# Graph network, four layers on one core: a 16-bit running table in the ranking, a longer late part, and 2 KB lines in the third node stage

## The reference, cut to what matters

```python
h = jnp.maximum(_layernorm(x, axis=-1), 0.0)
x = x + _L0_gnn_ref(h, edge_index, ...)   # needs scores[e] = a_s.h[src] + a_t.h[dst]
h = jnp.maximum(_layernorm(x, axis=-1), 0.0)
x = x + _L1_gnn_ref(h, src, dst, edge_weight, ...)
h = jnp.maximum(_layernorm(x, axis=-1), 0.0)
x = x + _L2_gnn_ref(h, src, dst, ...)     # softmax over the edges of one src, then sum into dst
h = jnp.maximum(_layernorm(x, axis=-1), 0.0)
x = x + _L3_gnn_ref(h, edge_index, edge_attr_2, ...)
```

## Time and profile before

| what | us |
|---|---|
| median of 3 runs (7792.51 to 7794.23) | 7792.8 |
| the profiled execution | 7779.12 |
| its span | 7777.4 |
| ranking: loop over 392 tiles, about 837 to 1409 | 572 |
| ranking: late part, about 1409 to 1523 | 114 |
| ranking: POOL alone, about 1523 to 1565 | 42 |
| node pass 2, about 3616 to 4475 | 859 |

### The profile page before, as it was taken

The page is one execution under the profiler, slowest core; times in us unless marked ns, Lnnn a source line. Parts: engine busy times, 40 slices in busy tenths (PEclk is TensorE's granted clock), DMA queues, the critical chain, the costliest instruction groups (busy, mean ns, idle before and its releaser), DMA issues. The chain is left out here.

```text
span 7777.4 us, 155361 instructions
## 1 busy us (share of the span) xinstructions
PE 5839.5 (75%) x23114; PEld 3656.9 (47%) x23115; DVE 5209.4 (67%) x18189; ACT 3315.6 (43%) x9563; POOL 3876.2 (50%) x4972
## 2 busy tenths in 40 slices
PE   4997999847779997677999967777686779400477
PEld 3774344336634443554444445555335668300365
DVE  5999777745579995455666656666784569533765
ACT  1993355205545552344444445454222557300155
POOL 1556777700022224766766677777460013577443
PEclk7999999979999998999999989999899999755799
DMA  2664333559867775787999866666208978422177
GB/s 59 211 211 129 101 104 103 170 164 337 307 213 247 249 248 196 248 309 259 308 305 306 290 196 205 204 204 202 63 7 280 339 252 228 130 54 55 50 234 249
DMA packets 970395, 1560.51 MB, mean 201 GB/s; under 512 B 125352, under 2 KB 736925, under 8 KB 970246
## 3 DMA queue, kind: packets, MB, share of 16 engines
q1 hardware_dynamic: 654502, 860.68, 33.7%
q10 hardware_dynamic: 188000, 410.91, 15.2%
q0 software_dynamic: 127744, 287.44, 13.5%
HBM read 861.17 MB, written 697.48 MB: 200 GB/s over the span
## 5 line engine op out<-in xcount | busy, mean ns | idle before, releaser
L2128 PE MATMUL node_p_out<-w,node_h_t 128*128 128x512 f32 (+2 forms) x6272 | 2176.8, 470 | 13.1 <-ACT node_h_t L2164 12.3
L1434 PE MATMUL merge_banks<-merge_rows,merge_mask 128*128 x6264 | 1537.5, 401 | 538.5 <-SPq L1365 139.8
L1434 PEld LDWEIGHTS merge_banks<-merge_rows,merge_mask 128*128 128x128 f32 x6264 | 1204.8, 198 | 871.2 <-issue 710.5
L1416 DVE TENSOR_SCALAR merge_mask<-ramp,dst_at,soft_at_step 128x128 f32<-128x128 f32 x2349 | 822.9, 353 | 778.0 <-PE merge_banks L1434 623.9
L2128 PEld LDWEIGHTS node_p_out<-w,node_h_t 128*128 128x128 f32 x6272 | 1013.9, 191 | 452.8 <-issue 396.9
L2041 POOL TENSOR_TENSOR node_inv_std<-node_var,node_minus_half 128x4 f32<-128x4 f32 x392 | 434.1, 1107 | 1428.9 <-DVE node_var L1926 857.4
L1498 ACT COPY merge_total<-merge_banks 128x512 f32<-128x512 f32 x784 | 458.1, 584 | 1097.0 <-PE merge_banks L1434 1014.4
L2106 PE MATMUL node_p_turn<-ident,node_xn 128*128 128x128 f32 x3136 | 620.6, 280 | 219.0 <-DVE node_xn L1933 116.4
L2106 PEld LDWEIGHTS node_p_turn<-ident,node_xn 128*128 128x128 f32 x3136 | 404.6, 141 | 768.2 <-issue 476.3
L2164 ACT ACTIVATE node_h_t<-node_p_turn 128x256 f32<-128x256 f32 x1568 | 601.3, 383 | 229.3 <-PE node_p_turn L2106 223.6
L1485 ACT COPY merge_banks<-merge_held 128x512 f32<-128x512 f32 x784 | 461.4, 589 | 228.2 <-PE merge_banks L1424 114.9
(11 more groups left out here) (564 smaller groups left out, 11073.3 us busy)
## 6 DMA issues: line engine op xcount, KB each, us to landing
merge_held<-own ACTq DMA_DIRECT2D x196, 512.0 KB, 6.0
x<-merge_total ACTq DMA_DIRECT2D x196, 512.0 KB, 4.3
node_x<-x SPq DMA_DIRECT2D x196, 512.0 KB, 6.1
node_x<-in_x SPq DMA_DIRECT2D x194, 512.0 KB
merge_rows<-h_by_edge SPq DMA_DIRECT2D x408, 128.0 KB, 4.2
merge_rows<-by_edge SPq DMA_DIRECT2D x408, 128.0 KB, 3.7
h<-node_rows_h SPq DMA_DIRECT2D x98, 516.0 KB, 4.2
h_by_edge<-rank_src_of_src SPq DMA_DIRECT2D x49, 1024.0 KB, 4.6
```

The source lines that it names most:

```text
L1416: ins = nc.vector.tensor_scalar(mask[j][:], k.ramp[:, 0:P], columns(k.dst_at, s), columns(weight, s), ALU.is_equal, ALU.mult)
L1434: nc.tensor.matmul(banks[:, bass.ds(nc.s_assert_within(at[2 * j + 1], 0, (BANKS - 1) * 512, skip_runtime_bounds_check_because=small), D)], ...
L2128: ins = nc.tensor.matmul(p_out[w][g % banks][:, 0:n], h_t[g][:, c * P:(c + 1) * P], matrix[:, c, :], start=c == 0, stop=c == 1)
```

## The change

In the loop the float32 snapshot and float32 look-up are replaced: `coarse` holds the table rounded to 16 bits (two copies, by block), `p_run` holds what is left over, which is small enough to be exact in 16 bits. `rank` becomes three 16-bit matmuls, and `copies` makes one 16-bit copy that `match` and `rank` both use. Before the first tile of each block DVE does three operations in a row (`take_apart`): add coarse to `p_run`, round the sum into the other coarse, put the difference back into `p_run`. `snap` of that tile waits for it. LATE goes from 15 to 19 blocks (152 tiles). The splitting of the late keys moves from ahead of the histogram to behind the loop. In node pass 2 `normalize` writes into `out`, where it stands beside the first product, and one DMA stores both as lines of 2 KB.

```diff
-    LATE = 15 * U
+    LATE = 19 * U
...
+            chain(nc.vector.tensor_tensor(whole, below[:], p_rank[1][:, 0:NTH], ALU.subtract))
+            chain(nc.vector.tensor_copy(coarse_of(0), whole))
             dve.sem_inc(prefix, 1)
+            nc.vector.tensor_tensor(p_run[:, 0:NTH], whole, coarse_of(0), ALU.subtract).then_inc(rebased, 1)
...
+            def take_apart(t, j):
+
+                if j or (isinstance(t, int) and t == 0):
+                    return
+                dve.wait_ge(added, t)
+                nc.vector.tensor_tensor(whole, p_run[:, 0:NTH], coarse_of(t - U), ALU.add).then_inc(rejoined, 1)
+                dve.wait_ge(rejoined, block_of_tile(t))
+                if not (isinstance(t, int) and t == U):
+                    dve.wait_ge(ranked, t - U)
+                nc.vector.tensor_copy(coarse_of(t), whole).then_inc(parted, 1)
+                dve.wait_ge(parted, block_of_tile(t))
+                nc.vector.tensor_tensor(p_run[:, 0:NTH], whole, coarse_of(t), ALU.subtract).then_inc(rebased, 1)
+
+            walk(dve, [(0, head), (2, before_in_tile), (2, take_apart), (4, pick)])
...
-                nc.tensor.matmul(p_rank[j % 2][:, 0:NTH], low_t[j][:], starts[j % FOUR][:], start=True, stop=False)
+                nc.tensor.matmul(p_rank[j % 2][:, 0:NTH], low_t[j][:], coarse_of(t), start=True, stop=False)
+                nc.tensor.matmul(p_rank[j % 2][:, 0:NTH], low_t[j][:], starts[j % FOUR][:], start=False, stop=False)
...
             def snap(t, j):
                 after(act, added, t)
+                if j == 0:
+                    act.wait_ge(rebased, block_of_tile(t) + 1)
                 after(act, ranked, t - FOUR + 1)
...
             def copies(t, j):
                 act.wait_ge(turned, t + 1)
-                after(act, same, t - FOUR + 1)
-                nc.scalar.copy(low_tb[j % FOUR][:], p_turn[j % 2][:, 0:P]).then_inc(copied_b, 1)
                 after(act, ranked, t - U + 1)
                 nc.scalar.copy(low_t[j][:], p_turn[j % 2][:, 0:P]).then_inc(copied, 1)
...
-                    parts = [out[q.h][:, n] for n in range(2)] + [biased[q.h][:], xn[q.h][:]]
+                    parts = [out[q.h][:, :, 0:2, :].rearrange("p g n f -> p g (n f)"), out[q.h][:, :, 2, :], biased[q.h][:]]
...
-                        nc.scalar.copy(out[q.h][:, 0:2, g, :], p_out[0][g % banks][:].rearrange("p (n f) -> p n f", n=2)
+                        nc.scalar.copy(out[q.h][:, g, 0::2, :], p_out[0][g % banks][:].rearrange("p (n f) -> p n f", n=2)
...
-        node_pass(nc, k, 2, x2, tables=(pair2[:, 0:D], to_dst, own2, pair2[:, D:2 * D]))
+        node_pass(nc, k, 2, x2, tables=(pair2, to_dst, own2))
```

More of the change, by code:

```diff
@@ L408, in rank_sources @@
     at_high = [ph.sb(f"at_high{n}", [P, NTH], BF16) for n in range(U)]
-    low_t = [ph.sb(f"low_t{n}", [P, P]) for n in range(U)]
-    low_tb = [ph.sb(f"low_tb{n}", [P, P], BF16) for n in range(FOUR)]
+    low_t = [ph.sb(f"low_t{n}", [P, P], F16) for n in range(U)]
     earlier = [ph.sb(f"earlier{n}", [P, P], BF16) for n in range(FOUR)]
-    starts = [ph.sb(f"starts{n}", [P, NTH]) for n in range(FOUR)]
-    counts, below, upto, zeros = starts
+    starts = [ph.sb(f"starts{n}", [P, NTH], F16) for n in range(FOUR)]
+    coarse = ph.sb("coarse", [P, 2 * NTH], F16)
+    scratch = ph.sb("scratch", [P, 4 * NTH])
+    late_low_t = [scratch[:, n * P:(n + 1) * P] for n in range(U)]
+    whole = scratch[:, 3 * NTH:4 * NTH]
+    counts, below, upto, zeros = (scratch[:, n * NTH:(n + 1) * NTH] for n in range(4))
     picked = [ph.sb(f"picked{n}", [P, NTH], BF16) for n in range(2)]
@@ L551, in pick @@
                     nc.vector.tensor_copy(columns(pos_out, t - U + 1, U), rank_f[:]).then_inc(rank_kept, 1)
-            walk(dve, [(0, head), (2, before_in_tile), (4, pick)])
+            def take_apart(t, j):
[10 more added lines that the diff above has]
+            walk(dve, [(0, head), (2, before_in_tile), (2, take_apart), (4, pick)])
+            late_part, late_high, late_low = (t[:, START:START + LATE] for t in (part_i, high, low))
+            late_key = columns(k.dst_i, START, LATE)
+            chain(nc.vector.tensor_scalar(late_part, late_key, 7, None, ALU.logical_shift_right))
+            chain(nc.vector.tensor_copy(late_high, late_part))
+            chain(nc.vector.tensor_scalar(late_part, late_key, P - 1, None, ALU.bitwise_and))
+            chain(nc.vector.tensor_copy(late_low, late_part))
             def late_head(m, j):
@@ L627, in late_look @@
                 pe.wait_ge(picked_n, NT + m - 1)
-                nc.tensor.matmul(p_rank[j % 2][:, 0:NTH], low_t[j][:], table[:, 0:NTH], start=True, stop=True).then_inc(ranked, 1)
+                nc.tensor.matmul(p_rank[j % 2][:, 0:NTH], late_low_t[j], table[:, 0:NTH], start=True, stop=True).then_inc(ranked, 1)
             walk_late([(0, late_turn), (1, late_look)])
@@ L1771, in node_pass @@
         own = both("own", [P, G, D])
-    xn = both("xn", [P, G, D])
+    xn = both("xn", [P, G, D]) if layer != 2 else None
     stats, moments = both("stats", [P, G, 6]), both("moments", [P, G, 2])
@@ L1776, in node_pass, with normal @@
     h_t = [ph.sb(f"h_t{n}", [P, D]) for n in range(G)]
-    out = both("out", {0: [P, 1, G, D + 3], 1: [P, 1, G, D], 2: [P, 2, G, D], 3: [P, 1, G, P + 8]}[layer])
+    out = both("out", {0: [P, 1, G, D + 3], 1: [P, 1, G, D], 2: [P, G, 3, D], 3: [P, 1, G, P + 8]}[layer])
     junk = [ph.sb(f"junk{n}", [P, D]) for n in range(2)]
+    def normal(side, g):
+        return out[side][:, g, 1, :] if layer == 2 else xn[side][:, g, :]
     p_turn = [ph.ps(f"p_turn{n}", [P, 512]) for n in range(2)]
```

34 lines of the change are left out of this document (16 added, 18 removed).

## The result

| | before | after |
|---|---|---|
| median, us | 7792.66 (7785.82 to 7794.23, 4 runs) | 7860.38 (7856.91 to 7866.3, 4 runs) |
| profiled execution, its span | 7779.12, 7777.4 | 7856.91, 7855.2 |

The ratio is 1.0092 (95% interval 1.008 to 1.0104): 0.9% slower. The forecast was 7795, range 7738 to 7824.

The account below looks back on a forecast made before the run. The prediction took a ring of waits through ACT to set the ranking loop's pace and POOL to bound the phase's end by 40 us. Sum: 7792.8 + 24 (ranking) - 22 (node pass 2) = 7795 us, range 7738 to 7824.

Parts of the forecast that it names:

- The ring: Ranking loop: each tile step is a ring of waits, `add`, `turn`, ACT's copies, `snap`, next `add`, 1.39 us before the change.
- the plain step of 1.23: Ranking loop: dropping one of ACT's two copies, 0.16 us a tile, makes the step 1.23 us.
- `take_apart` at 2.0 us: Ranking loop: three chained DVE operations ahead of `snap` add 2.0 us a block, bounds 1.6 and 2.4.
- PE then has six 16-bit matmuls a tile: Ranking loop: at most 0.17 us each, 1.02 in all, below 1.23, so PE's saving is worth nothing more.
- a clock below 0.99 in the new pauses: Ranking loop: sign that the prediction is wrong, PE's clock falling below 0.99 in new pauses of some 2 us.
- the loop's term: Ranking loop: 48 blocks get longer by 35 us in all, range +16 to +55.
- the forecast block of 12.28: Ranking loop: a block of 8 tiles takes 8 x 1.23 + 0.44 (branch) + 2.0 = 12.28 us, range 11.9 to 12.7.
- The late part, +30: Ranking behind the loop: 32 more tiles looked up late on DVE, picks 0.94 us apart, add 30 us.
- POOL's end at about 1525: Ranking's end: four blocks lose their `of_dst` gathers, -37 us; POOL ends near 1525, covered by DVE.
- Node pass 2, -22 (0 to -39): Node pass 2: stores land 0.45 us sooner, once in two groups, 49 times, -22 us; range 0 to -39.
- the slow stretch: Node pass 2: stores at 263 GB/s from 3999.0 to 4001.5; if `xn`'s short lines cause it, 0.8 us gained.
- B: Slower case: the stores' slow stretch belongs to x's load, issued one issue earlier, so no stores' gain; 7817 us, chance 0.26.

Follow-up runs that it names:

- experiments 2 and 3: 2: changed kernel, table parted once ahead of the loop, 0.9919. 3: changed kernel, ten constant PE matmuls before each block's first `add`, 1.0043. Ratios to the kernel before.
- `e9_split`: Kernel before, ranking untouched, with node pass 2's new SBUF layout but four stores of 1 KB lines; ratio 0.997 to the kernel before.
- `e1_lines`: Kernel before, ranking untouched, with only the change's node pass 2 part (lines of 2 KB, three stores); ratio 0.998 to the kernel before.
- the kernels of the table that gain: Three kernels before with node pass 2's normalized rows at another place and four stores kept; ratios 0.9982, 0.9963 and 0.997 to the kernel before.
- experiment 5: Changed kernel with `take_apart` ahead of the one-hot and mask on DVE; 7842 us, ratio 1.0059 to the kernel before.
- experiment 4: Changed kernel with five matmuls on constants ahead of each block's first `add`; 7830 us, ratio 1.0063 to the kernel before.
- experiment 6: Changed kernel with `take_apart` cut to one DVE operation, the remainder put right by two PE matmuls; 7795 us, ratio 1.0001 to the kernel before.
- `e14_xn_last`: Kernel before with node pass 2's normalized rows in their own buffer, allocated behind out and the scratch buffers; ratio 0.9982 to the kernel before.

## Why the prediction was wrong

By its own steps:

- **The ring and the plain step of 1.23.** Right: 1.22 in every run where PE had its clock. The branch costs a little more, 10.42 a block instead of 9.84 + 0.44 = 10.28.
- **`take_apart` at 2.0 us.** A little small, within its bounds: experiments 2 and 3 give 12.71 - 10.42 = 2.29 in the blocks shown, and (614.1 - 507.5)/48 = 2.2 over the loop. The first operation started 1.07 after `add`, not 0.82; from there to `snap` it took 1.86 (1011.33 to 1013.19), forecast 1.77.
- **"PE then has six 16-bit matmuls a tile, ... its saving is hidden behind the ring."** This is the step that failed. It holds at 2.4 GHz only. Behind nearly every pause PE runs at or near half of that, its six matmuls take 1.52 us against the ring's 1.22, and three steps cost 13.65 - 12.71 = 0.94 us more a block. The prediction named a clock below 0.99 in the new pauses among what would make it wrong, and gave it neither a price nor a case. So the loop's term was +35, bounded at +55, and measured +95. In loop times: the forecast block of 12.28 makes 600.2 over 391 steps, 660.5 were measured, and of the 60.3 between them 46.4 are the clock (660.5 - 614.1), 8.9 the parting (614.1 - 507.5 - 48.9 x 2.0) and 5.1 the branch (507.5 - 48.9 x 10.28).
- **The late part, +30.** Right: 139.5 us from first to last late pick for 152 tiles, against 111.6 for 120, +28.
- **POOL's end at about 1525, covered.** Near enough, and covered: last gather 1530.0, then 113.6 us of waiting.
- **Node pass 2, -22 (0 to -39).** Measured -14 in the trace of after and -0.2% (16 us) alone. The landing went from 7.85 to 7.50 us (first store issued at 4002.43, join at 4009.93), and PE's 49 waits for `normalize` from 1.27 to 0.95 us in the mean, (69.6 - 22.9)/49, which is 15 us. The size was near; its reason was wrong, and that is luck. The gain belonged neither to the length of the lines nor to the place of x's load among the issues, since `e9_split` has four stores of 1 KB lines ahead of that load, as before, and gains as much. The first 1 MB landed at 4.25 us with lines of 2 KB (`e1_lines`) and at 4.32 with lines of 1 KB (`e9_split`). Only a part of the slow stretch went: the fourth store took 2.24 us behind the third before, and 1.74 to 1.93 in the kernels of the table that gain, against 1.2 to 1.4 for the second and third.
- **The cases.** The time lies above B, which was the case without any gain from the stores; no case held a block of more than 12.7 us.

## What to carry to other kernels

Where a change puts a pause (1.2 to 2.2 us here) into a loop that keeps PE busy, price the steps behind the pause at half the clock too: take the matmuls of a step, double the distance from one start to the next (0.17 became 0.33 us here), and see whether they still fit under the ring. If they don't, cut the pause or put idle matmuls into it; here ten of them gave back 46 us of a loop of 660. And before a gain is put down to the form of a transfer, run one version with the same addresses and the old form, and read the landing of each store for itself.

## What was not expected of the hardware

- A pause of 2.17 us once in 13.6 brought the granted clock to 0.57 for the 3.3 us behind it, while in the pause itself the rows give 1.00; pauses of 1.78 us still did so in 41 of 48 blocks (experiment 5), of 1.24 us in 25 of 48 (experiment 4), and two of 0.51 and 0.65 us in 9 of 47 (experiment 6).
- Moving the four buffers of the normalized rows (4 KB a partition each) behind all others, which shifts those in between by 16 KB, with the same instructions and the same DMAs, changed a pass of 98 groups from 825 to 807 us and its DMA rate from 306 to 314 GB/s; the store of those rows landed 0.35 us sooner, the others 0.04 to 0.06 (`e14_xn_last`).
- A matmul with a bf16 stationary and an fp16 moving operand ran like the others, 0.34 us for 392 columns (experiment 6).
